# Two native key tiles a batch instead of four, and the maxima of a query group taken directly behind its third chunk

## The reference

```python
x = x + xattn(layernorm(x), ctx, Wq, Wk, Wv, Wout, bout)      # softmax(q k^T / 8) v, then Wout
x = x + ffn(layernorm(x), clip_x, clip_down, w_gate, w_up, w_down)
...
xq = fake_quant(x, clip_x)                                   # scale from the largest |x| of all tokens
h = fake_quant(silu(xq @ q(w_gate).T) * (xq @ q(w_up).T), clip_down)
return h @ q(w_down).T
```

## Time and profile before

| | us |
|---|---|
| median of three timed runs | 200.93 (200.44 to 202.4) |
| profiled execution | 200.77 |
| its span, first to last instruction | 199.0 |
| granted TensorE clock, mean | 0.981 |

### The profile page before, as it was taken

The page is one execution under the profiler, slowest core; times in us unless marked ns, Lnnn a source line. Parts: engine busy times, 40 slices in busy tenths (PEclk is TensorE's granted clock), DMA queues, the critical chain, the costliest instruction groups (busy, mean ns, idle before and its releaser), DMA issues.

```text
span 199.0 us, 2722 instructions
## 1 busy us (share of the span) xinstructions
PE 187.1 (94%) x867; PEld 141.7 (71%) x867; DVE 149.3 (75%) x349; ACT 115.2 (58%) x240; POOL 104.0 (52%) x94
## 2 busy tenths in 40 slices
PE   7689998999999999999989999999899999989782
PEld 2565475888888888888868788887678878856330
DVE  3356799868895986698968857889689509996684
ACT  2245685665776674667656746676565366642532
POOL 5858775545455652585546525855464265641020
PEclk9957999999999999999999999999999999999999
DMA  6963471015105200520043005200010000000001
GB/s 153 214 148 106 143 199 50 2 28 169 39 0 131 86 16 0 127 93 15 2 128 106 2 0 146 86 4 0 0 39 0 3 0 2 2 0 3 0 0 46
DMA packets 11638, 11.38 MB, mean 57 GB/s; under 512 B 8288, under 2 KB 9488, under 8 KB 11624
## 3 DMA queue, kind: packets, MB, share of 16 engines
q1 hardware_dynamic: 10824, 10.38, 19.5%
q10 hardware_dynamic: 800, 0.83, 2.0%
HBM read 10.96 MB, written 0.23 MB: 56 GB/s over the span
## 4 chain that ended last, share of the span: by engine, by line
PE 72%; DVE 12%; DMA 7%; ACT 3%; POOL 2%; issue 1%; SPq 0%; POOLq 0%; DVEq 0%; ACTq 0%
PE p_m L821 11%; PE p_o L856 10%; PE p_s L839 9%; PE p_s L834 8%; PE p_s L835 8%; PE p_o L868 6%; PE p_o L863 5%; PE p_o L865 5%; DMA ctxT_in<-ctxT_d 5%; PE p_x L874 3%; DVE chunk_max L510 2%; PE p_s L913 2%; DMA q_hi<-maxima 2%; DVE ctx_lo L504 2%; POOL e_lo L306 2%; PE p_o L913 1%
## 5 line engine op out<-in xcount | busy, mean ns | idle before, releaser
L306 POOL TENSOR_TENSOR e_lo<-e_full,e_hi 125x448 fp32r<-125x448 f32 x64 | 82.1, 1285 | 66.9 <-ACT e_full L407 66.6
L510 DVE TENSOR_REDUCE chunk_max<-p_m 112x1 f32<-112x500 f32 x96 | 63.8, 675 | 27.2 <-PE p_m L821 25.2
L405 ACT ACTIVATE e_hi<-p_s 125x448 fp32r<-125x448 f32 x64 | 34.9, 546 | 36.9 <-PE p_s L839 36.0
L834 PE MATMUL p_s<-q_hi,ctxT_lo 96*125 96x448 f32 x96 | 45.9, 478 | 0.0
L821 PE MATMUL p_m<-ctxT_hi,q_hi 96*112 96x500 f32 x96 | 38.5, 421 | 1.4 <-DVE chunk_max L510 0.9
L839 PE MATMUL p_s<-q_hi,ctxT_hi 97*125 97x448 f32 x96 | 35.6, 371 | 1.5 <-DMA q_hi<-maxima 1.5
L835 PE MATMUL p_s<-q_lo,ctxT_hi 96*125 96x448 f32 x96 | 35.1, 365 | 0.0
L407 ACT ACTIVATE e_full<-p_s 125x448 f32<-125x448 f32 x64 | 34.4, 538 | 0.0
L856 PE MATMUL p_o<-e_full,ctx_nat 125*128 125x448 f32 x64 | 29.4, 540 | 0.0
L410 ACT ACTIVATE e_full<-p_s 125x448 f32<-125x448 f32 x32 | 17.4, 544 | 16.7 <-PE p_s L839 16.7
L863 PE MATMUL p_o<-e_hi,ctx_hi 125*128 125x448 f32 x64 | 23.9, 373 | 0.0
(11 more groups left out here) (197 smaller groups left out, 210.8 us busy)
## 6 DMA issues: line engine op xcount, KB each, us to landing
ctxT_in<-ctxT_d SPq DMA_DIRECT2D x8, 562.5 KB, 4.7
ctx_in<-ctx_d SPq DMA_DIRECT2D x8, 375.0 KB
ctx_nat<-ctx_d SPq DMA_DIRECT2D x8, 187.5 KB
q_hi<-maxima SPq DMA_DIRECT2D x28, 0.4 KB, 1.9
wqT<-wqT_d SPq DMA_DIRECT2D x1, 256.0 KB, 4.3
wout<-wout_d ACTq DMA_DIRECT2D x1, 256.0 KB, 10.3
x_in<-x_in_d SPq DMA_DIRECT2D x1, 224.0 KB, 2.8
wkT<-wkT_d ACTq DMA_DIRECT2D x1, 192.0 KB, 3.5
```

What stands on the lines that cost most here:

```text
L306: pool.tensor_tensor(e_lo[:, k, :], e_full[:, k, :], e_hi[:, k, :], ALU.subtract)\
L405: act.activation(e_hi[:, k, :], p_s[n % 2][0:KT, 0:HQ], ACT.Exp, scale=SCALE)\
L510: dve.reduce_max(chunk_max[:, c // NM, c % NM:c % NM + 1], p_mb[c % NM][0:GQ, 0:MC], AX.X)\
L834: pe.matmul(o, ctxT_lo[b % 2][:, keys], q_hi[0:C, b, :], start=True, stop=False)
```

## The change

Tiles 2 and 8 of each batch become split: 10 split and 2 native tiles. With it `ctx_in`, `ctx_hi` and `ctx_lo` hold 10 tiles (a half is 5 tiles, 480 columns instead of 384), `ctx_nat` 2. The bytes that are loaded stay the same. On VectorE each group's maxima stand directly behind the reduction of its third chunk, ahead of the tile's other work, and `layernorm2` stands in tile 9 instead of 8.

```diff
-NATIVE = (2, 5, 8, 11)
+NATIVE = (5, 11)
...
                     at = chunks_at(b, t)
                     for nb, c in at:
                         chunk(nb, c)
+                        if c % NM == NM - 1:
+                            group(nb, c // NM)
                     if t <= 2 and b + 1 < B:
                         split_ctxT_lo(b + 1, t)
...
-                    if b % 2 and b >= 3 and t == 8:
+                    if b % 2 and b >= 3 and t == 9:
                         layernorm2((b - 3) // 2)
-                    for nb, c in at:
-                        if c % NM == NM - 1:
-                            group(nb, c // NM)
```

## The result

The changed kernel takes 205.81 us (median of four runs, 205.33 to 207.41; a fifth took 204.88), the kernel before 201.39 (four runs, 200.44 to 202.4). The ratio is 1.022, with a 95% interval of 1.015 to 1.030: **slower by 2.2%**, where 198.5 was forecast. The profiled execution took 207.41 (span 205.6, mean granted clock 0.950, against 199.0 and 0.981).

The account below looks back on a forecast made before the run. The prediction took TensorE, busy in 94% of the span, to bound the kernel. Its terms, -2.0 - 2.0 + 0.5 + 0.2 + 1.0 = -2.3 us against 200.77, gave 198.5, with a range from 197.1 to 200.5.

Parts of the forecast that it names:

- A tile on TensorE: In TensorE's chain, each native tile made split saves about 0.14 us; 14 counted, -2.0 us.
- The maxima: In batches 3 and 5, the score matmul's two 1.0 us stalls for the maxima's DMA go whole: -2.0 us.
- Holds in the batches, +0.5: Added e_lo hold VectorE, so projections of batches 4 and 6 come up to 0.35 us later each; bounds 0 and 2.3.
- The start, +0.2: In batch 0, two wider ctx_lo on VectorE take 0.1 us more each; +0.2 us, bounds 0 and 1.15.
- The end, +1.0: In batch 7, tile 8's new e_lo delays all behind it, VectorE's last normalisation included: +1.0 us, bounds 0 and 2.3.
- tile 2's also shifts the quantisation: In batch 7, tile 2's e_lo also delays VectorE's weight quantisation: the case behind the end's upper bound, 2.3 us.
- Rival D: GpSimd becomes the bound in the batches, deciding only from 1.8 us per e_lo: some 205 us; chance 0.07.
- Rival A: Holds by e_lo eat more, at the projections 2.3 instead of 0.5 us: 200.3 us; chance 0.22.
- C: The maxima don't get earlier in the batches, so only the tiles count: 200.4 us; chance 0.08.
- B: The end costs nothing, VectorE's burst fitting where GpSimd is idle: 197.2 us; chance 0.13.

Follow-up runs that it names:

- e1: The changed kernel with four native tiles a batch again, so only the new order on VectorE differs from the kernel before: 199.88 us, ratio 0.992.
- e16: The kernel before, four native tiles kept, but with ctx_in, ctx_hi and ctx_lo of 10 tiles (480 columns a half): 202.49 us, ratio 1.002.
- e5: The changed kernel with tiles 2 and 8 native again in batch 0 only, ctx_lo still 480 columns: 204.91 us, ratio 1.012.
- e10: The changed kernel with twelve unused matmuls of 512 columns on TensorE ahead of the waiting chunk matmul in batch 0: 202.92 us, ratio 1.000.
- e2: The kernel before with two native tiles a batch instead of four, old order on VectorE kept: 206.82 us, ratio 1.022.
- e3: The changed kernel with VectorE's xb and sig operations moved from ahead of the first chunk to behind batch 0: 200.49 us, ratio 0.995.
- e4: The changed kernel with VectorE's quantisation of the weights moved from behind batch 7 to behind batch 6: 205.25 us, ratio 1.013.

## Why the prediction was wrong

- **A tile on TensorE: right.** Six tiles took 8.86 to 8.91 (8.85 forecast). The sign was right as well: three split products are cheaper than one native.
- **The maxima: right.** Both waits of the earlier trace rows went, and e1 alone gives the 2.0.
- **Holds in the batches, +0.5: right in size.** The waits of the projections grew from 0.8 to 1.6 (1.3 forecast), and the whole stretch from tile 5 of batch 0 on came to -3.48 against -3.5. That it agrees so closely is in part luck: the stretch has 15 of the new split tiles where 14 were counted (-2.2 instead of -2.0), and the projections took 0.8 instead of 0.5.
- **The start, +0.2: the step that failed, mostly.** It came to 5.0. I costed the wider `ctx_lo` by its columns (0.1 each) and took the earlier trace rows to say that VectorE's burst goes first and GpSimd waits. In that row the two engines were in contention already, and who goes first there was an outcome that a change of width could reverse. It did (1.1, by e16). The second error was to place tile 2's `e_lo` behind those operations because it had been there: once the first `e_lo` no longer stands in line, it comes early enough to catch `sig` (1.0, by e5). My upper bound of 1.15, one more hold, was one short. The third error cost the most: I took a wait of TensorE at its length. The kernel before ran at 2.4 GHz throughout the batches; I had no row of what comes behind a longer wait, and no term for it. It was 2.9, by e10 (1.4 to 4.6 in the profiles with that wait).
- **The end, +1.0 (bounds 0 and 2.3): wrong in size and in place.** It came to 3.1. I looked for the loss at the last `e_lo`, behind the quantisation. But tile 2's `e_lo` and tile 8's met the small operations ahead of it, each of which can be held by a whole `e_lo`, or by two: 0.17 became 2.01. I had reasoned on bursts of long operations and left out the short ones. The sign of a second loss was in the bound ("tile 2's also shifts the quantisation"), at 1.15 where the queue shows 2.8, and 0.4 for the clock. TensorE's wait of 2.2 for `wd_q` was in none of the prediction's signs. In e2 and e3 the same tiles cost 1.6, inside the bounds: which of the two sizes comes was not to be read from the rows before.
- **The rivals.** Rival D gave 205, near the time measured, for a wrong reason: `e_lo` has a mean of 1.29 us, far from the 1.8 from which it decides, and inside the forecast's own 1.2 to 1.35. Rival A had the right mechanism and the wrong places: it put the losses at the projections, and all its upper bounds together reach 202.6, short of the clock. C and B fell.
- **The range** (197.1 to 200.5) left out the case in which start and end reach their upper bounds together, though both hang on the same cause. But even all upper bounds together give 202.6: the bounds of start (1.15 against 5.0) and end (2.3 against 3.1) were too small in themselves.

The Trainium skill ("SBUF — State Buffer", SBUF: two separate sides) calls the shared pair of ports an exclusive lock: whichever of the two instructions starts first has it for the whole instruction, and the other is fully blocked. The rows agree: `xb` 0.68 or 1.67, `sig` 0.15 or 1.10, with nothing between in the profiles. What it leaves open is who is next when both stand in line, and by e4 that need not be the one that has waited longest.

The Trainium skill ("TensorE: Matmul & The Clock Gate", The HAM clock gate) gives TensorE two clocks, 1.2 and 2.4 GHz. The trace agrees, with 0.50 and 1.00 in the stretches above and matmuls of 0.37 and 0.21. Its figure for the price, under 1% of a typical kernel's span, is for the ramp at the start, which no run here prices; one fall in mid-kernel, behind a wait, was 2.9 us here, 1.4%.

## What to carry to other kernels

Where two engines exclude each other, the cost of one more operation is read operation by operation: each short one on the other engine, however small, can be held for a whole long one or several, and rows in which contention is already visible are an outcome that a change of width or of what follows can turn round. Ask of each wait that grows on TensorE whether it will let the clock fall, and put that in the range. When such a wait appears, the cheap repair is to move what nobody wants yet out from ahead of the operation that is waited for; here it was worth more (5.3 us) than the whole change was meant to bring.

## What the runs showed of the hardware

- Behind a wait of 3.0 us TensorE's granted clock fell to 0.50 in all four profiles that have it, but for about 3, 7, 7 and 10 us; the cost was 1.4 to 4.6 us (2.9 between the medians of the changed kernel and e10). Behind 2.0 it fell in both profiles that have that wait (e5, e16), behind 2.2 near the end in two of three (not in e10), behind 0.9 and 1.1 it stayed at 1.00. Twelve matmuls without use in the gap of 3.0 kept it at 1.00.
- Instructions that queue up on GpSimd without a gap can keep a VectorE operation out for several of them: 4.07 us for one of 0.39, 2.01 for a copy of 0.17. The same copy took 0.88 and 0.89 in e3 and e2. And VectorE's operations back to back kept an `e_lo` out.
- Who gets in between two VectorE operations of one burst turned with their width (384 to 480 columns: 1.01 to 2.19) and with what stands behind them (`xb` or `ctxT_lo`: 1.01 or 1.97), and was the same in every profile of kernels with the same start (four, ten and three). A delay of 0.27 us did not turn it. The rule behind this stays open.
